# A four-layer graph network on one core: row factors of the attention layers moved to PSUM, half of a count two steps later, and the loops over graphs written out

## The reference, cut to what matters

```python
x = _layernorm(x + _L0_gnn_ref(adj, x, W, b))   # max over each node's first 25 neighbours, then a projection
x = _layernorm(x + _L1_gnn_ref(x, adj, ...))     # graph attention ("gat 1")
x = _layernorm(x + _L2_gnn_ref(x, adj, W, a))    # graph attention ("gat 2")
x = _layernorm(x + _L3_gnn_ref(x, adj, ...))     # softmax(q x^T + mask), used in two steps with tanh
# inside a graph attention layer:
f1 = Wh @ a1
f2 = Wh @ a2
e = leaky_relu(f1[:, :, None] + f2[:, None, :], 0.2)
attention = softmax(where(adj > 0, e, -9e15), axis=2)
h_prime = einsum('bij,bjo->bio', attention, Wh)
return elu(h_prime)
```

## Time and profile before

| | us |
|---|---|
| median of three runs | 2056.16 |
| profiled execution | 2046.86 |
| its span | 2045.1 |
| TensorE busy | 1712.1 (84%) |
| VectorE busy | 1458.2 (71%) |
| ScalarE busy | 1017.3 (50%) |
| GpSimd busy | 1536.4 (75%) |

### The profile page before, as it was taken

The page is one execution under the profiler, slowest core; times in us unless marked ns, Lnnn a source line. Parts: engine busy times, 40 slices in busy tenths (PEclk is TensorE's granted clock), DMA queues, the critical chain, the costliest instruction groups (busy, mean ns, idle before and its releaser), DMA issues.

```text
span 2045.1 us, 30121 instructions
## 1 busy us (share of the span) xinstructions
PE 1712.1 (84%) x9310; PEld 1300.3 (64%) x9364; DVE 1458.2 (71%) x3543; ACT 1017.3 (50%) x1353; POOL 1536.4 (75%) x2202
## 2 busy tenths in 40 slices
PE   2757698898889898897889898897989988896877
PEld 1535477576766677575765677575766777575745
DVE  5767588677887688677886678767886778845531
ACT  3010465457555465557645555655654574642152
POOL 5888888888878887888878887888878888881000
PEclk9878899998999899998999989998999989997889
DMA  6331222424233422423232532423223342311010
GB/s 157 90 73 46 74 74 72 123 76 111 79 99 82 121 71 69 126 74 100 73 108 85 123 79 69 125 74 98 73 71 120 84 98 63 101 42 39 1 62 11
DMA packets 154433, 169.44 MB, mean 83 GB/s; under 512 B 103261, under 2 KB 120554, under 8 KB 154282
## 3 DMA queue, kind: packets, MB, share of 16 engines
q1 hardware_dynamic: 119594, 96.43, 17.6%
q0 software_dynamic: 34688, 71.11, 13.2%
HBM read 142.81 MB, written 4.19 MB: 72 GB/s over the span
## 4 chain that ended last, share of the span: by engine, by line
PE 43%; DVE 17%; POOL 17%; issue 7%; ACT 5%; DVEq 4%; DMA 4%; SPq 1%; another core or an unknown queue 1%; ACTq 0%; POOLq 0%
POOL gathered L521 13%; PE spare L840 8%; PE big L942 7%; POOL pause L526 4%; PE big L1072 4%; PE big L1020 4%; PE side L1052 3%; PE big L1036 3%; DMA adj_t<-adj_bf 2%; PE side L840 2%; DVEq L72 2%; DVE probs_t L1372 2%; PE big L866 2%; DVE pooled L1246 2%; PE big L933 2%
## 5 line engine op out<-in xcount | busy, mean ns | idle before, releaser
L521 POOL DMA_INDIRECT gathered<-in_x_dram,rows x1084 | 1148.6, 1060 | 270.2 <-issue 163.0
L526 POOL MEMSET pause<- 32x256 bf16 x1084 | 383.1, 353 | 42.0
L840 PE MATMUL spare<-hot,x_part 128*128 128x512 f32 x1312 | 345.3, 418 | 44.0 <-DVE hot L1293 43.3
L840 PEld LDWEIGHTS spare<-hot,x_part 128*128 128x128 f32 x1312 | 258.5, 201 | 106.2 <-issue 31.5
L582 ACT ACTIVATE hot<-running,minus_count 128x2048 fp32r<-128x2048 bf16 x105 | 209.8, 1998 | 56.3 <-PE spare L840 56.3
L1246 DVE TENSOR_REDUCE pooled<-gathered 128x128 f32<-128x2176 f32 (+2 forms) x56 | 219.0, 3912 | 19.9 <-DMA gathered<-in_x_dram,rows 17.3
L942 PEld LDWEIGHTS big<-values,probs_t 128*128 128x128 f32 x1792 | 225.8, 204 | 9.0
L942 PE MATMUL big<-values,probs_t 128*128 128x129 f32 x1792 | 228.6, 288 | 1.0 <-issue 0.9
L1293 DVE TENSOR_SCALAR hot<-running 128x2048 fp32r<-128x2048 bf16 x153 | 187.9, 1253 | 43.9 <-PE spare L840 32.2
L585 ACT ACTIVATE hot<-hot,plus_one 128x2048 fp32r<-128x2048 f32 x105 | 210.3, 2002 | 3.4
L840 PE MATMUL side<-hot,x_part 128*128 128x512 f32 x560 | 154.8, 427 | 60.4 <-ACT hot L585 42.2
(11 more groups left out here) (195 smaller groups left out, 2539.1 us busy)
## 6 DMA issues: line engine op xcount, KB each, us to landing
adj_in<-in_adj_dram SPq DMA_DIRECT2D x128, 512.0 KB, 3.9
gathered<-in_x_dram,rows POOLq DMA_INDIRECT x1084, 2.5
xs<-in_x_dram SPq DMA_DIRECT2D x8, 512.0 KB, 4.4
out_dram<-xs SPq DMA_DIRECT2D x8, 512.0 KB, 3.5
adj_t<-adj_bf SPq DMA_TRANSPOSE x64
packed_t<-group_bits SPq DMA_TRANSPOSE x28
w_sb<-in_L_gnn_W_dram SPq DMA_DIRECT2D x1, 128.0 KB
w_sb<-in_L_gnn_W_dram SPq DMA_DIRECT2D x2, 64.0 KB
```

Source lines behind the costliest of these rows:

```text
L521: (late_gathered if late else rows_gathered[t % RING]).raised_by(pool.indirect_dma_start(out=gathered[:, t % RING, k * C:(k + 1) * C], out ...
L526: last = nc.gpsimd.memset(pause[quarter:quarter + 32, k // (4 * PAUSED), :], 0.0)
L840: last = nc.tensor.matmul(pick_bank(b, q), x_parts[part][:, m, :], hot[c][:, m % per, :], start=(m == 0 and part == 0), stop=(m == T - 1 a ...
```

## The change

Four edits:

1. `row_gain` (SBUF) is gone. ScalarE writes the row factors into `side` (PSUM, both banks; named `gains`), and VectorE reads them there. Because `side` also holds the value sum, ScalarE copies `value_sum` out first and waits for that copy.
2. Pick 6 leaves `BESIDE`, so it goes to `spare`. It waits for the maximum of pick 4 in place of `sum_ready`.
3. `spare` is now taken until the maximum of pick 6. VectorE takes that maximum after the third `probs_t` instead of after the eighth, and TensorE starts the counts of the second half after j = 2 instead of j = 0; the last two j carry two counts each.
4. The loops over graphs are written out on all five engines.

```diff
-BESIDE = (1, 5, 6, 8, 14)
+BESIDE = (1, 5, 8, 14)
...
-        row_gain = sb("row_gain", [P, N])
-        queries = row_gain
+        queries = sb("queries", [P, N])
...
+        gains = side[:, :]
...
-            with sp.Fori(0, LOOPED // 2) as two:
-                graph(two * 2, 0, True)
-                graph(two * 2 + 1, 1, True)
-            for b in range(LOOPED, B):
+            for b in range(B):
                 graph(b, b % 2, False)
...
-            with pool.Fori(1, B) as b:
+            for b in range(1, B):
                 for t in range(T):
                     gather(b, t)
...
-                row_gain_ready.raised_by(nc.scalar.activation(row_gain[:, :], low, ACT.Exp, scale=1.0 - NEG_SLOPE,
+                act.wait_ge(sum_psum.sem, sum_psum.at(b, layer))
+                sum_ready.raised_by(nc.scalar.copy(value_sum[:, 0:C], side[0:1, 512:512 + C]))
+                act.wait_ge(sum_ready.sem, sum_ready.at(b, layer))
+                row_gain_ready.raised_by(nc.scalar.activation(gains, low, ACT.Exp, scale=1.0 - NEG_SLOPE,
                                                               bias=row_shift[:, 0:1]))
                 value_gain_ready.raised_by(nc.scalar.activation(
                     values[:, :, C:C + 1].rearrange("p t a -> p (t a)"), col_gap[:, :], ACT.Exp))
-                act.wait_ge(sum_psum.sem, sum_psum.at(b, layer))
-                sum_ready.raised_by(nc.scalar.copy(value_sum[:, 0:C], side[0:1, 512:512 + C]))
...
                     else:
-                        pe.wait_ge(sum_ready.sem, sum_ready.at(b, layer))
+                        spare_maxed(b + 1, 4)
                         pick(b + 1, 6)
...
+                        if layer == 2 and j >= T - 2 and t == HALF - 1 and exists(b, 1, B, in_loop):
+                            count(b + 1, 1 - slot, 1, 2 * j - T)
...
-                    if layer == 2 and exists(b, 1, B, in_loop):
-                        if j == 0:
-                            spare_maxed(b + 1, 4)
-                        count(b + 1, 1 - slot, 1, j)
+                    if layer == 2 and j >= 2 and exists(b, 1, B, in_loop):
+                        if j == 2:
+                            spare_maxed(b + 1, 6)
+                        count(b + 1, 1 - slot, 1, j - 2 if j < T - 2 else 2 * j - T + 1)
...
-                        out=probs_t[:, j, :], in0=row_gain[:, :], scalar=col_gain[:, j:j + 1],
+                        out=probs_t[:, j, :], in0=gains, scalar=col_gain[:, j:j + 1],
                         in1=adj_t[slot][:, j, :], op0=ALU.max, op1=ALU.mult))
-                if picks:
-                    max_pick(b + 1, 2 if layer == 1 else 6)
+                    if picks and layer == 2 and j == 2:
+                        max_pick(b + 1, 6)
+                if picks and layer == 1:
+                    max_pick(b + 1, 2)
```

More of the change, by code:

```diff
@@ L150, in build_graph_layers @@
     GP = P // GROUP
-    LOOPED = B - 2
     TOP = tops(1)
-    assert C == P and T == 2 * HALF and LOOPED % 2 == 0
+    assert C == P and T == 2 * HALF
     x_rows = x.rearrange("b n c -> (b n) c")
@@ L243, in build_graph_layers @@
         b1_rep = work[:, 1, 0:P]
-        group_key_i = row_gain[:, 0:G].bitcast(I32)
+        group_key_i = queries[:, 0:G].bitcast(I32)
         values = sb("values", [P, T, C + 1])
@@ L756, in _ @@
                 take_count(1, 0, j)
-            with act.Fori(0, LOOPED // 2) as two:
-                graph(two * 2, 0, True)
-                graph(two * 2 + 1, 1, True)
-            for b in range(LOOPED, B):
+            for b in range(B):
                 graph(b, b % 2, False)
@@ L1126, in _ @@
             count_first(1, 1)
-            with pe.Fori(0, LOOPED // 2) as two:
-                graph(two * 2, 0, True)
-                graph(two * 2 + 1, 1, True)
-            for b in range(LOOPED, B):
+            for b in range(B):
                 graph(b, b % 2, False)
@@ L1532, in _ @@
             dve.wait_ge(setup_done, 3)
-            with dve.Fori(0, LOOPED // 2) as two:
-                graph(two * 2, 0, True)
-                graph(two * 2 + 1, 1, True)
-            for b in range(LOOPED, B):
+            for b in range(B):
                 graph(b, b % 2, False)
```

## The result

The changed kernel took 2034.8 us (median of 4 executions, 2026.6 to 2035.6) beside 2059.6 us for the kernel before (4 executions, 2053.4 to 2065.3). The ratio is 0.9871, with a 95% interval of 0.9830 to 0.9913. The forecast of 2044 was for a ratio of 0.994, so the gain of 24.8 us is twice the 12.5 forecast. The two profiled executions lie closer together: 2046.86 us before and 2035.60 after, where the sum for the profiled execution gave 2034.4.

What follows compares the result with a forecast made beforehand. VectorE bounds short gat 2 stages, TensorE's late pick 6 the long ones, GpSimd limits afterwards. Terms -4 - 12 + 3.5 = -12.5 took 2056.2 to 2043.7, say 2044 us; range 2032 to 2058, forecast's own 2038 to 2050.

Steps and rivals of the forecast that it cites:

- Pick 6 without its wait: Gat 2, TensorE: pick 6 starts 1.91 to 2.05 us earlier, shortening four long stages; -12 us, bounds -13.6 and -7.0.
- The clock step: Gat 2: without stillness before pick 6, its first stretch at clock 0.50 may go too, worth 1.6 us.
- Value sum ahead: Attention layers: ScalarE's earlier copy makes products begin 0.3 us later; +3.5 us (gat 2 2.1, gat 1 1.4), bounds 0 and +4.8.
- Row factors in PSUM: VectorE's products stay at 1277 ns; GpSimd's gathers beside them shorten, but its wait for tile 1 swallows that; 0 us.
- Loops written out: Jumps back after graphs 1 and 3: their stalls go, 3.7 us by layer 0, 4.7 by the chain; taken -4.
- Give-back in the attention: Attention stage: GpSimd limits from gat 2's reduction to the graph's end, taking back 0.3 us per shortened gat 2.
- sign of being wrong: Attention stages longer than 107.2 us would mean that another bound stands behind them.
- More to gain than the profile shows: Rival, chance 0.17: all seven gat 2 stages are long in timed runs, so -23.5 us: 2033.
- Clock falls all the same: Rival, chance 0.23: in gat 2 the clock still falls, so only -7.5 us in all: 2049.
- The loops' stalls: Rival, chance 0.07: fetching written-out code holds the engines as often as the jumps did: 2048.
- The products were not slower: Rival, chance 0.05, claimed VectorE's products are slower reading PSUM, +3 us and +1.4 for the write: 2048.
- the maximum of pick 6: Rival, chance 0.06: in gat 2 VectorE waits 2.4 us for a slow pick 6, delaying products; +10.3 us: 2066.5.

Runs made afterwards that it cites:

- series two: Second set of kernels run one after the other on one chip (chip 11): before 2038.2 us, changed 2022.6 us, ratio 0.9915.
- pick waiting: Changed kernel with TensorE again waiting for ScalarE's row factors before pick 6; ratio to the kernel before 0.9933, on repeating 0.9988.
- loops alone: Kernel before with only its loops over graphs written out on all engines; ratio 0.9923 (2038.4 us), on repeating 0.9883.
- GpSimd's loop out: Kernel before with only GpSimd's loop over graphs written out; ratio 1.0015, +3.1 us.
- the others out: Kernel before with the loops of SyncE, ScalarE, TensorE and VectorE written out and GpSimd's kept; ratio 0.9975, -5.1 us.
- series three: Third set of kernels run one after the other on one chip (chip 13): before 2090.3 us, changed 2087.3 us, ratio 1.0011.
- series one: First set of follow-up kernels, run one after the other on one chip, testing parts of the change; kernel before 2056.7 us.

## Why the prediction was right or wrong

**Pick 6 without its wait: right for gat 2.** Forecast -12 us, bounds -13.6 and -7.0. The eight gat 2 stages give 13.0 us in the profile of series two and 7.9 in the first one of the changed kernel; that includes what the later products cost, so it stands against -12 + 2.1 = -9.9. The wait is gone in all seven graphs, and the reciprocal waits in none of seven in series two, and 1.20 and 0.76 us in two of seven in the first profile. The clock step is supported, but as a chance and not a rule: pick 6 took 5.5 us in 16 of 42 graphs where TensorE had stood still 1.5 to 2.2 us before it (before 4 of 7, pick waiting 4, loops alone 1 and 0, GpSimd's loop out 4, the others out 3; the profile of the pick-waiting kernel in series three left out), and never more than 4.7 us in 41 graphs of the six profiles in which pick 6 comes without idle time. The wait put back brought four long stages back. What the prediction left out is that a long gat 2 stage is largely made good elsewhere: those 13.3 us cost the profiled execution 2.4.

**Value sum ahead, +3.5 us: right in its mechanism.** The products of gat 2 begin 13.3 to 13.6 us into the stage in series two, against 12.9 to 13.3 before: 0.3 us later. Its price is measured by no run: gat 1, where I had put 1.4 us, did not grow (400.9 and 397.7 us in sum against 401.1).

**Row factors in PSUM, 0: right for the products, refuted for the time in series three.** 1276 against 1277 and 1278 ns, and 1.09 us for ScalarE's write in either place (1.12 in series three, to SBUF). By the 65 ns more per instruction that the Trainium skill (Perfetto Trace Analysis, Optimizing Scalar/DVE Operations) gives, the median would have been about 1342, an estimate from that page; the measurement decides. Gathers became 0.95 us and GpSimd's wait grew, to 5.9 to 14.5 us where I said 11: swallowed, as forecast. But the only direct test, in series three, puts the factors in PSUM 35 us behind SBUF, where the bounds allowed +4.4 us. It was made once, on one chip, and its cause is open; in series one the edits that include it still gained 9.5 us.

**Loops written out, -4 us: the mis-sized term.** The stillness at the jumps was read rightly (1.98 us again in series one). But all loops out measured -15.8 and -24.5 us in series one and three, and their two parts -5.1 and +3.1 in series two. The step that failed is the term of -4, read off one execution: "by the layer 0 stages the loss is [...] together 3.7; by the chain 4.7". It took what stands at two jumps for the cost of the loops. The 15.8 - 4 = 11.8 us more are nearly the whole distance from 12.5 to 24.8. Where they lie stays open: layer 0 in graphs 2 and 4 gives 5.8 and 6.7 us in the two clean pairs of profiles, but is as short in a kernel that keeps the jumps.

**Give-back in the attention, 0.3 us a stage: about right in sum, not stage by stage.** Graphs 3 and 4 take 107.2 and 107.1 us. All eight stages together grew by 2.3 us in the first profile of the changed kernel and by 1.0 in series two, against 4 x 0.3 = 1.2. Graph 1 took 108.9 and stages of series two up to 107.6, above the 107.2 that was named as a sign of being wrong.

**The rivals.** "More to gain than the profile shows" named 2033, and 2034.8 was measured, but not for its reason. It wanted all seven gat 2 stages long in the timed runs; no profile of any kernel with the wait had more than four, and series two timed the kernel before at 2038.2, below the profiled 2046.86. No run shows its reason, so that 2034.8 came near 2033 counts as chance. "Clock falls all the same" was half true: the clock fell behind pick 6 in five of seven gat 2 stages of the first profile, and in four of these the reciprocal had no wait all the same (in graph 1 it waited 1.20 us). The loops' stalls did not stay: written out alone, the loops gave 15.8 and 24.5 us, and no issue gap is left where the jumps were. The products were not slower, and the maximum of pick 6 never waited for TensorE (in graph 0 VectorE stood 1.50 us before it, more than 3 us after pick 6 had ended).

So the term of pick 6 and the size of the whole in the profiled execution came out near the forecast, and the timed gain did not. That the time fell inside the range owes something to luck: the loops gave four times their share in series one, and in series three the whole change gave nothing.

## What to carry to other kernels

A wait of two microseconds on TensorE can lengthen its stage by 3.6: look at the granted clock behind it before pricing it, and then look at what the later stages give back. A stall that one profile shows at a jump did not tell what the loops cost (15.8 and 24.5 us in two series, about 2 by parts in a third); write the loops out alone and time that, beside the full change. Before a gain under 1.5% is believed, run the old kernel in more than one series: here it moved by 52 us, and the change was worth 27 us or nothing.

## What the runs showed of the hardware that I had not expected

In the profile of the changed kernel in series three TensorE ran in bursts. Its weight loads in gat 1 of graph 1, and GpSimd's gathers at the same time:

```profile
534.28 0.52 PEld L936 LDWEIGHTS big<-values,probs_t 128*128 128x128 f32 x4 [0.34 <-issue]
535.71 0.52 PEld L936 LDWEIGHTS big<-values,probs_t 128*128 128x128 f32 x4 [0.90 <-issue]
...
537.13 0.52 PEld L936 LDWEIGHTS big<-values,probs_t 128*128 128x128 f32 x4 [0.52 <-issue]
```

```profile
533.98 0.95 POOL L517 DMA_INDIRECT gathered<-in_x_dram,rows  x1 [0.16 <-issue]
...
535.43 0.95 POOL L517 DMA_INDIRECT gathered<-in_x_dram,rows  x1 [0.16 <-issue]
...
536.88 0.95 POOL L517 DMA_INDIRECT gathered<-in_x_dram,rows  x1 [0.16 <-issue]
```

Four groups of loads start 1.42 to 1.46 us apart (four to seven loads each, then a pause), close to the 1.45 us from gather to gather; after them 24 loads run without a pause. In series two the 48 loads at this place run as one group:

```profile
514.09 5.55 PEld L936 LDWEIGHTS big<-values,probs_t 128*128 128x128 f32 x48
```

The line of the page for them, series three and then series two, beside the 9.6 us of the first profile above:

```profile
L936 PEld LDWEIGHTS big<-values,probs_t 128*128 128x128 f32 x1792 | 237.7, 210 | 32.0 <-issue 23.6
```

```profile
L936 PEld LDWEIGHTS big<-values,probs_t 128*128 128x128 f32 x1792 | 219.8, 199 | 8.6
```

23.6 us of idle time in which nothing in the profile was waited for, on this line alone, against none. In series three the same line of the pick-waiting kernel, also with its factors in PSUM, has 19.8 us; the two profiled kernels with theirs in SBUF have 0.6 us (loops alone) and none. But both profiles with bursts are of executions slower than the median of their kernel, 2105.14 us against 2087.3 and 2111.83 against 2088.9, so the bursts may belong to those executions and not to the series. The rhythm suggests that TensorE is held by what the gathers do, and steadier gathers would then hold it more often; that would also fit the 35 us between the two places of the row factors in that series. It is an argument only: the changed kernel of series two has the same steady gathers and no bursts, and the kernel before, with its factors in SBUF, was just as slow on that chip and was not profiled there. What sets the level of a series, whether these bursts are TensorE's supply of instructions, and whether PSUM plays a part in them, stays open.
